# Attention and routed experts on one core: choice and routing in fifteen steps, token tiles finished in pairs inside the attention bodies

## The reference

```python
xn = _layernorm(x, axis=-1)
# s: causal attention with ALiBi, 32 query heads, 16 key/value heads, head size 64
qkv = xn @ W_qkv
scores = einsum(q, k) / sqrt(64) + slope[h] * (kpos - qpos)
s = softmax(where(causal, scores, -inf)) @ v ... @ W_out
# f: each token goes to its 2 best of 8 experts (512 hidden units each)
gate_logits = xn @ gate_w + gate_b
topk_vals, topk_idx = top_k(gate_logits, 2)
topk_w = softmax(topk_vals)
f = sum over the two of topk_w * (gelu(xn @ w1[e] + b1[e]) @ w2[e] + b2[e])
out = x + s * silu(f)
```

## Time and profile before

| what | before |
|---|---|
| median of 3 runs | 1232.81 us (1229.16 to 1232.95) |
| the profiled execution's own time | 1230.63 us |
| its span, first to last instruction | 1228.8 us |
| PE busy | 1128.3 us, 92% |
| DVE busy | 994.0 us, 81% |
| ACT busy | 927.5 us, 75% |
| POOL busy | 873.5 us, 71% |
| mean granted clock of PE | 0.968 of 2.4 GHz |

### The profile page before, as it was taken

How to read it: one execution, slowest core, us unless ns; L and a number is a source line. 1 busy time by engine, 2 the same in 40 slices (tenths; PEclk the granted TensorE clock), 3 DMA queues, 4 the chain that set the end, 5 groups by cost and what they waited for, 6 DMA issues and landing times. The chain is left out here.

```text
span 1228.8 us, 51239 instructions
## 1 busy us (share of the span) xinstructions
PE 1128.3 (92%) x16970; PEld 832.7 (68%) x16970; DVE 994.0 (81%) x3099; ACT 927.5 (75%) x1808; POOL 873.5 (71%) x1082
## 2 busy tenths in 40 slices
PE   2578999999999999998998889999999999999994
PEld 1355776676777777776887656777777777777773
DVE  8768888888888888884777767888888888888875
ACT  3356888888888888886666567888888888888883
POOL 8036899999998888885000057888888888888886
PEclk8579999999999999999999989999999999999997
DMA  8324666655566555565434255655555555555554
GB/s 264 142 56 87 131 132 132 138 128 126 138 126 130 128 127 128 128 133 92 88 88 113 65 136 120 125 122 119 119 119 119 119 119 119 119 119 119 119 121 95
DMA packets 267759, 148.89 MB, mean 121 GB/s; under 512 B 172946, under 2 KB 256242, under 8 KB 266996
## 3 DMA queue, kind: packets, MB, share of 16 engines
q1 hardware_dynamic: 263540, 138.85, 50.9%
q0 software_dynamic: 4096, 8.40, 2.4%
HBM read 15.76 MB, written 16.78 MB: 26 GB/s over the span
## 5 line engine op out<-in xcount | busy, mean ns | idle before, releaser
L792 POOL TENSOR_TENSOR t_lo<-stage 128x512 f16<-128x512 f32 x640 | 654.4, 1038 | 174.8 <-ACT stage L1198 172.0
L1462 DVE CUSTOM_DVE_ANT_0 stage<-ps,kmask 128x512 bf16<-128x512 f32 (+3 forms) x1024 | 451.7, 488 | 108.5 <-PE ps L891 83.7
L1198 ACT ACTIVATE stage<-ps,slope 128x512 f32<-128x512 f32 (+1 forms) x768 | 440.0, 618 | 96.0 <-PE ps L928 83.5
L919 PE MATMUL ps<-q_st,k_st 128*128 128x256 f16 (+3 forms) x1024 | 300.7, 303 | 12.7 <-issue 5.4
L951 PE MATMUL outs<-v_sp,stage 128*128 128x65 f16 x2560 | 263.9, 195 | 7.1 <-POOL t_lo L792 6.5
L953 PE MATMUL outs<-v_sp,stage 128*128 128x64 f16 x2560 | 262.7, 194 | 0.0
L955 PE MATMUL outs<-v_sp,t_lo 128*128 128x65 f16 x2560 | 262.7, 194 | 0.0
L951 PEld LDWEIGHTS outs<-v_sp,stage 128*128 128x128 bf16 x2560 | 235.8, 98 | 29.9 <-issue 14.6
L953 PEld LDWEIGHTS outs<-v_sp,stage 128*128 128x128 bf16 x2560 | 236.0, 99 | 0.0
L955 PEld LDWEIGHTS outs<-v_sp,t_lo 128*128 128x128 f16 x2560 | 235.7, 98 | 0.0
L920 PE MATMUL ps<-q_st,k_st 128*128 128x128 f16 x1024 | 224.2, 219 | 0.0
(11 more groups left out here) (205 smaller groups left out, 2665.9 us busy)
## 6 DMA issues: line engine op xcount, KB each, us to landing
q_st<-stage SPq DMA_DIRECT2D x256, 128.0 KB, 2.4
k_st<-stage SPq DMA_DIRECT2D x128, 128.0 KB
q_st<-stage SPq DMA_DIRECT2D x256, 64.0 KB, 2.1
k_st<-stage SPq DMA_DIRECT2D x128, 64.0 KB
slot_y<-stage SPq DMA_DIRECT2D x40, 128.0 KB, 2.0
X<-in_L_attn_inputs SPq DMA_DIRECT2D x8, 512.0 KB, 8.5
slot_x<-att SPq DMA_DIRECT2D x2, 2048.0 KB, 8.7
wx_raw<-in_L_ffn_w SPq DMA_DIRECT2D x64, 64.0 KB
```

The source lines that it names most:

```text
L792: pool.tensor_tensor(t_lo[r], t_p[r], upper(t_p[r]), ALU.subtract).then_inc(s[f"lo{u % NG}"], 1)
L919: pe.matmul(d, k[:, 0, at], q[:, 0, seen], start=(c0 == 0), stop=False, skip_group_check=True)
L1198: e = act.activation(t_p[r][:, c0:c1], S_ps[u % 2][:, c0:c1], ACT.Exp, scale=slope[:, bass.ds(pair_index(n) * 2 * SLOTS + sl * 2 + h, 1)])
L1462: ins = dve.tensor_tensor_reduce(junk[h][:, c0:c0 + w], M_ps[h][:, c0:c0 + w], kmask[:, SEQ - w:SEQ], -1.0 / 1024, 3e38, ALU.add, ALU.min, ...
```

## The change

What it does, by engine:

- PE: the gate products of a batch follow the transposes of a later batch; the ranks' products move from V0 of body 1 to C0 of body 0, ahead of the first window. PE, ACT and DVE no longer wait for the output weights' split before the bodies.
- DVE: `choose` has six steps (after B1, B3, B5, B7, B9, B11 of body 0) and `route` nine: six in body 1's maxima (B3 to B11) and N0 of body 0, three later (N0 of bodies 4, 6, 8). The output weights' remainder is gone from DVE, and the end is laid out anew.
- POOL: in body 0 the four quarters of the output weights' remainder stand after L1, L3, L5, L7; the five operations on `b2` follow at L9 of body 0, L1, L4, L6 and L9 of body 1. Both slot numbers of a tile are copied by one operation. In the second half three operations of 128x256 finish a pair of tiles (U0, U1, U2) every second window.
- ACT: the output weights are scaled by a second pass; silu(f) becomes f * (0.5 + 0.5 * tanh(f / 2)), with a tanh and a linear activation (T0) of 128x256 per pair of tiles inside the bodies.
- Sends: first with body 2, double in bodies 5 and 8; the unrolled part of the first half so ends at window 10.
- SP stores each finished pair inside the bodies (H0); the last four tiles are stored by SP and ACT, two tiles each.

```diff
         "ACT": [
-            ("V0", 1, 35), ("K0", 2, 38), ("E4", 0, 42), ("F1", 0, 46), ...
+            ("V0", 1, 35), ("K0", 2, 38), ("T0", -3, 38), ("E4", 0, 42), ("F1", 0, 46), ...
         "POOL": [
-            ("L0", 0, 10), ("L1", 0, 18), ("G0", -1, 25), ("L2", 0, 27), ("L3", 0, 34), ("I0", 1, 41),
-            ("L4", 0, 47), ("I1", 1, 54), ("L5", 0, 56), ("L6", 0, 63), ...
+            ("L0", 0, 10), ("U2", -4, 10), ("L1", 0, 18), ("G0", -1, 25), ("L2", 0, 27), ("U0", -3, 27), ("L3", 0, 34), ("I0", 1, 41),
+            ("L4", 0, 47), ("L5", 0, 56), ("U1", -3, 56), ("L6", 0, 63), ...
...
-        FIRST_ONES = {"DVE": [("B1", 0), ("B3", 0), ("B5", 0), ("B3", 1), ("B5", 1), ("N0", 0), ("B3", 2), ("B5", 2),
-                              ("N0", 1), ("B3", 3), ("B5", 3)],
-                      "PE": [("V0", 1)], "ACT": [("E4", 0)]}
-        CHOICES = 3
+        FIRST_ONES = {"DVE": [("B1", 0), ("B3", 0), ("B5", 0), ("B7", 0), ("B9", 0), ("B11", 0),
+                              ("B3", 1), ("B5", 1), ("B7", 1), ("B9", 1), ("N0", 0), ("B11", 1),
+                              ("N0", 4), ("N0", 6), ("N0", 8)],
+                      "PE": [("C0", 0)], "ACT": [("C1", 0)],
+                      "POOL": [("L1", 0), ("L3", 0), ("L5", 0), ("L7", 0), ("L9", 0), ("L1", 1), ("L4", 1), ("L6", 1), ("L9", 1)]}
+        CHOICES = 6
...
-        FIRST_SENT, TWICE = 4, (7, 10, 13, 16)
+        FIRST_SENT, TWICE = 2, (5, 8)
...
+                if k < O_STEPS:
+                    pool.wait_ge(s["wo_hi"], 1)
+                    pool.tensor_tensor(lo, wo_in[:, c], hi, ALU.subtract).then_inc(s["wo_lo"], 1)
...
+            def finish(n, par, k):
+                if par == 0 or not finishes(n):
+                    return
+                if k == 0:
+                    pool.wait_ge(s["tangent"], pairs)
+                    pool.wait_ge(s["acc"], n)
+                    pool.tensor_tensor(m, m, tiles_of(att, t), ALU.mult).then_inc(s["summed"], 1)
+                elif k == 1:
+                    pool.wait_ge(s["sigmoid"], pairs)
+                    pool.tensor_tensor(m, m, g_pair, ALU.mult).then_inc(s["gated"], 1)
+                else:
+                    pool.tensor_tensor(tiles_of(X, t), tiles_of(X, t), m, ALU.add).then_inc(s["fin"], 1)
...
             for q in range(1, NB):
                 turn_inputs(q)
-            pe.wait_ge(s["xlo"], NB)
+                if q >= 4:
+                    gate_products(q - 4)
+            for q in range(NB - 4, NB):
+                gate_products(q)
...
-            split_lo(O_PART)
-            weights_split(dve)
-            finish(dve, 2)
+            leave_bodies("DVE", tasks, HALF, BODIES, late=[BODIES - 1])
+            dve.tensor_tensor(a, a, m, ALU.mult).then_inc(s["partial"], 1)
+            dve.tensor_tensor(xx, xx, a, ALU.add).then_inc(s["partial"], 1)
+            dve.wait_ge(s["op"], BODIES)
+            for c in range(2):
+                dve.scalar_tensor_tensor(out=a[:, cols], in0=bank_of("O0")[:, cols], scalar=1.0 / WS, in1=m[:, cols],
+                                         op0=ALU.mult, op1=ALU.mult).then_inc(s["fresh"], 1)
+                dve.tensor_tensor(xx[:, cols], xx[:, cols], a[:, cols], ALU.add).then_inc(s["fin_last"], 1)
```

More of the change, by code:

```diff
@@ L817, in _ @@
             leave_bodies("POOL", fetches, HALF, BODIES)
-            finish(pool, 0)
+            last = tiles_of(mix, LAST, QT)
+            pool.wait_ge(s["sigmoid"], LAST // 2 + 1)
+            pool.tensor_tensor(last, last, g_last[:, :], ALU.mult).then_inc(s["gated"], 1)
         @block.tensor
@@ L999, in _ @@
                 mm = pe.matmul(d, xT_lo[:, tok], gw16[:, 0, :], start=False, stop=True)
[L1000 to L1001 removed]
+                if t == NT - 1:
+                    mm.then_inc(s["gate"], 1)
+            for q in range(1, NB):
+                if q > 4:
+                    pe.wait_ge(s["xlo"], q - 3)
+                turn_inputs(q)
+                if q == 4:
+                    pe.wait_ge(s["gate_w"], 1)
+                if q >= 4:
+                    gate_products(q - 4)
+            for q in range(NB - 4, NB):
+                gate_products(q)
             def ranks(_):
@@ L1159, in v_hi_part, with gates @@
                                ACT.Copy, scale=1.0 / WS).then_inc(s["vh"], 1)
-            def gates(c):
-                g = out_chunk(mix, c)
-                act.activation(g, g, ACT.Silu).then_inc(s["silu"], 1)
-            def out_hi(n, _, sl):
-                final = isinstance(n, int) and (n, sl) == (BODIES - 1, 1)
-                if final:
-                    act.wait_ge(s["added"], NT)
-                    for c in range(2):
-                        gates(c)
+            def gates(n, par, _):
+                if finishes(n):
+                    t, pairs = pair_of(n, par)
+                    if par == 0:
+                        act.wait_ge(s["added"], t + 2)
+                        need(act, "gated", pairs - 1)
+                        act.nop(nofuse=True)
+                        act.activation(g_pair, tiles_of(mix, t), ACT.Tanh, scale=0.5).then_inc(s["tangent"], 1)
+                    else:
+                        act.wait_ge(s["tangent"], pairs)
+                        act.activation(g_pair, g_pair, ACT.Identity, bias=half[:, 0:1], scale=0.5).then_inc(s["sigmoid"], 1)
+            def out_hi(n, _, sl):
                 act.wait_ge(s[f"nrm{sl}"], n + 1)
@@ L1178, in out_hi @@
                 act.copy(by_head(a16[sl][:, 0:SEQ]), values_of(sl)).then_inc(s[f"ah{sl}"], 1)
-                if final:
-                    gates(2)
             def shifts(n, _, sl):
@@ L1317, in _ @@
             act.preload_act_table(ACT.Exp)
-            run_bodies(act, "ACT", {**tasks, "F": weigh}, HALF, BODIES)
+            run_bodies(act, "ACT", {**tasks, "F": weigh, "T": gates}, HALF, BODIES)
             leave_bodies("ACT", {**tasks, "F": weigh}, HALF, BODIES)
+            act.wait_ge(s["added"], NT)
+            act.activation(g_last[:, :], tiles_of(mix, LAST, QT), ACT.Tanh, scale=0.5).then_inc(s["tangent"], 1)
+            act.wait_ge(s["tangent"], LAST // 2 + 1)
+            act.activation(g_last[:, :], g_last[:, :], ACT.Identity, bias=half[:, 0:1], scale=0.5).then_inc(s["sigmoid"], 1)
+            act.wait_ge(s["fin_last"], 2)
+            act.dma_start(ot[:, LAST + QT // 2:NT, :], X[:, LAST + QT // 2:NT, :]).then_inc(s["outd"], 16)
         @block.vector
```

254 lines of the change are left out of this document (141 added, 113 removed), and 2 rows, old and new, of the table ORDER.

## The result

| | before | changed |
|---|---|---|
| median | 1232.81 us (1229.16 to 1235.02, 5 runs) | 1222.99 us (1221.62 to 1223.62, 5 runs) |
| profiled execution: own time, span | 1230.63, 1228.8 us | 1221.62, 1219.8 us |
| POOL, ACT, DVE busy in it | 873.5, 927.5, 994.0 us | 887.7, 935.9, 991.8 us |
| mean granted clock | 0.968 | 0.976 |

The ratio is 0.9922, with a 95% interval of 0.9901 to 0.9943. The direction was forecast, but the gain was 9.8 us (9.0 in the two profiled spans) where some 18 were expected. 1222.99 us lies outside the forecast's own range (1209 to 1218) and at the very edge of the wide one (1205 to 1223).

A forecast was written before the change was run, and what follows sets the result against it. TensorE, busy for all 15.10 us of a full-flow body, was taken as the bound. Start -9.4, sends -0.2, finishing +0.8 and end -9.1 made -17.9 us, so 1213.8 us; own range 1209 to 1218, wide range 1205 to 1223.

The forecast's parts named there:

- the 0.8 for meetings: First bodies: added 0.8 us, about one more VectorE operation lengthened by GpSimd's reads than before.
- Gate products and choice: Before body 0's row copies: products between transposes save 2.8 us, expert choice in six pieces saves 1.3.
- Ranks: Between body 0's row turn and body 1's first rough score: ranks' products add 3.1 us, clock at either level.
- -2.7 of 24.85: First long body: stall of 4.1 and ten operations go, eighteen of 6.9 us come, 1.0 in existing waits.
- rival of start-up collisions: Body 0: eight two-input VectorE steps meet GpSimd, 5.2 us, ranks at 1.2 GHz; 1218.5 us; chance 0.17.
- The third loses 2.0 of its excess: Third long body: routing change removes 2.0 us of its 2.2 us excess.
- So it has room: GpSimd, busy 10.46 of 24.85 us in body 0, can take four weight splits and five one-partition operations.
- The three late steps lie in bodies 4 to 8, where VectorE has 1.9 us free: Bodies 4 to 8: three late routing steps fit into VectorE's free time of 1.9 us.
- Sends: First half: two double bodies fewer, -2.6 us, eight bodies more in the loop, +2.4; together -0.2.
- Second half: Finishing tiles inside the bodies adds 0.8 us in all, between 0 and +6.
- The end: After the last bodies: earlier copy, projection and 128 KB store; with issue and final wait 1219.7, so -9.1 us.
- marks for being right: Signs: last DMA under 2.5 us after projection, maxima near 42.3, no 4 us VectorE stall, bodies about 22, 16, 15.3.

The follow-up runs named there:

- E3: Changed kernel with the output weights split by ScalarE and VectorE before the bodies again, nothing of it on GpSimd: 1219.63 us, 0.9896 of the kernel before.
- E6: Changed kernel with five routing steps (last two of body 0, three late ones) moved behind the query split TensorE waits for: 1216.03 us, 0.9876 of before.
- E2: Changed kernel with GpSimd's five bias operations back before the bodies, directly behind the clearing of att: 1219.06 us, 0.9893 of the kernel before.
- E12: Changed kernel with four bias operations right behind the clearing of att and the fifth after the seventh input remainder: 1216.83 us, 0.9883 of the kernel before.
- E1: Changed kernel with VectorE instead of GpSimd multiplying the last four tiles by their gates: 1220.66 us, 0.9908 of the kernel before.
- E4: Changed kernel with two of the three late routing steps moved to the half's last two bodies, the third in body 4: 1226.20 us, 0.9949 of before.
- E8: E6 and E1 combined, plus bias operations before the bodies but behind VectorE's small operations: 1210.18 us, 0.9837 of the kernel before.
- E9: E8 with the bias operations ahead of the clearing of att: 1210.38 us, 0.9828 of the kernel before.
- E10: E9 with the first routing steps, too, behind the splits that TensorE waits for: 1209.31 us, 0.9832 of the kernel before.
- E5: Kernel before, with only both slot numbers of a tile copied by one operation: 1230.48 us, 0.9992 of the kernel before.
- E7: Changed kernel with routing steps over bodies 0 to 3, first send in body 4 and four double bodies, as before: 1217.50 us, 0.9892 of before.

## Why the prediction was wrong, and what in it was right

The step that failed is the routing in the first bodies: its terms took the steps by length and by VectorE's free time, where their place in the queue and the GpSimd operations beside them decided. Its terms, put to the positions at which they can be read (differences to before, in us; the fourth row copies take the 0.8 for meetings in):

| up to | forecast | measured |
|---|---|---|
| row copies 0 (gate products, choice) | -4.1 | -5.5 |
| 1 (ranks, first long body) | -3.7 | -2.0 |
| 2 | -8.2 | -6.0 |
| 3 | -9.4 | -4.0 |
| 31 (sends, late steps) | -9.6 | +0.3 |
| 36 | -9.6 | -4.6 |
| 63 (finishing) | -8.8 | -3.1 |
| end | -17.9 | -9.0 |

- *Gate products and choice*: right and a little too small; 1.3 us came from a meeting that went with the bias operations.
- *Ranks*: 3.1 us, about the middle of the two clock levels, were taken; at the lower one they took 3.75. But the text booked them ahead of body 0 and then expected body 0 at "about 22", while they lie behind its row copies; by its own terms the mark should have been 25.
- *"-2.7 of 24.85"* for the first long body is the step that failed first: body 0 grew by 3.5 us, without the ranks' 3.75 that is -0.2. Two terms were mis-sized. The eighteen operations, "6.9 in all", took 10.8 us, of which 5.9 us are nine meetings with GpSimd; for meetings the sum had "0.8". And "1.0 of them falls into waits that are there" did not ask what stands behind the steps: the query splits, for which TensorE waited 3.1 and 4.7 us. The rival of start-up collisions, with its 0.17, foresaw this mechanism and its size on VectorE (eight meetings, 5.2 us). How much of the 5.9 us reached TensorE is measured only in part: E3 gives 1.8 us to the four weight pieces, E6 3.0 us in body 0 alone to the place of two steps. The clock was on the whole no lower than before (0.80, 0.88 and 1.00 in bodies 0 to 2, against 0.77, 0.92 and 0.93).
- *"The third loses 2.0 of its excess"*: it took 19.3 us where 15.3 were expected. "So it has room" counted GpSimd's busy time over body 0, where the prediction should have asked what stands in its queue ahead of the first send. E2 and E12 show the 4.3 us.
- *"The three late steps lie in bodies 4 to 8, where VectorE has 1.9 us free"*: free time is not free at that place. Bodies 4 to 8 lost 8.3 us, where one double body's 1.3 had been lost before and two doubles come to 2.6; E6 brings 4.1 back by place alone.
- *Sends*: two doubles fewer and eight bodies more in the loop cancel, as said.
- *Second half*: +1.5 over 27 bodies for 0.8; its beginning, for which nothing was forecast, gained 4.9, mostly together with a granted clock of 1.00 instead of 0.90. For the forecast this is luck: more than half of the 9.0 us measured comes from there, and without it the change would have gained 4.1.
- *The end*: -9.1 forecast, -5.9 measured. The chain up to the last store was right to a microsecond (the copy 16.5 us behind the last row copies instead of 15.4; last store issued 1.8 us after the projection). "With issue and final wait" missed GpSimd's closing drain: E1 shows 2.4 us.
- Of the marks for being right, the store (1.8 us behind the projection), the first rough maxima (41.0) and the missing stall ahead of the ranks' reader came, the body lengths did not: 28.3, 16.4 and 19.3 us for 22, 16 and 15.3. Of the marks for being wrong, small VectorE operations of 1 us came in numbers.

By the Trainium skill (SBUF — State Buffer, "Who interferes with whom") not only instructions with two SBUF inputs but also copies, casts and tensor_scalar in a two-port mode exclude a GpSimd instruction, of any kind, while reductions never do. The prediction used only the first half of this. The rows of E4, E8 and E9 agree with the other half (one-input operations of 32, 128 and 28 columns at 2.91, 1.0 and 2.78 us, the last beside a memset), and so does the reduction of 0.29 us in body 0; whether those operations ran in such a mode the traces do not say.

## What to carry to other kernels

A step costs what stands behind it in its queue, not its length: put small work right behind the operation that the bounding engine waits for, not ahead of it; here that alone was worth 6 us (E6). It ends where the next output that is waited for stands behind the moved work instead: E10 kept 0.3 of 1.8 us. Free time of an engine in a window says nothing of whether its next needed output is late. And small VectorE work costs as much as the GpSimd operation, or the unbroken row of them, that it meets, so look at both timelines side by side before moving it.

## What was not expected of the hardware

- A VectorE operation of 0.18 us was held for 2.91 us, through the last three of six gapless GpSimd operations (E4), and for 2.78 us by a memset (E9). GpSimd operations on a single partition hold it as well (1.55 us, E2).
- GpSimd's closing drain ended 9.2 us behind its last operation in the changed kernel and in the twelve versions that send as it does, and 7.9 us in the three kernels that send first with body 4 and double four times (before, E5, E7). It is part of the measured time unless it is covered. What sets its length stays open.
- The same matmuls of three bodies (640 or 641 records) took 47.77, 46.23 and 43.53 us in three kernels, at mean granted clocks of 0.90, 0.93 and 1.00; differences of 2 us in one stretch of single profiled executions are not evidence for an edit.
